# A fused mLSTM and FP4 feed-forward kernel: input rows of two batches in one transfer each, without copies of the inputs in DRAM

## The reference

```
q = layernorm(x); k = v = ctx
ig, fg = gates: [q, k, v] @ igate_w.T + igate_b, [q, k, v] @ fgate_w.T + fgate_b
log_f_cum = cumsum(log_sigmoid(fg)); log_D[s,t] = log_f_cum[s] - log_f_cum[t] + ig[t]  (t <= s)
D = exp(log_D - max_t log_D); C = (q k^T / 8) * D
h = C / (max(|sum C|, exp(-max)) + 1e-6) @ v; h = layernorm over each head * norm_w
x = x + h
z = layernorm(x); gate = fp4(z) @ fp4(w_gate).T; y = fp4(z) @ fp4(w_up).T      (512 -> 1408)
x = x + fp4(silu(gate) * y) @ fp4(w_down).T                                   (1408 -> 512)
```

## Time and profile before

| | |
|---|---|
| three runs | 2225.77, 2227.67, 2230.52 us (median 2227.67) |
| profiled execution | 2230.32 us, span in the trace 2228.6 us |
| mean granted TensorE clock | 0.902 of full speed |
| busy share of the span | PE 79%, DVE 81%, ACT 52%, POOL 55% |
| DMA | 647726 packets, 259.86 MB, mean 117 GB/s |

### The profile page before, as it was taken

One profiled execution on the slowest core, in us unless ns is written; L12 is line 12 of the kernel. 1 busy time (PEld: TensorE's weight loads), 2 busy tenths in 40 slices (PEclk: granted clock), 3 DMA queues, 4 the chain that ended last, 5 costly groups with the idle time before them and its releaser, 6 DMA issues. The chain is left out here.

```text
span 2228.6 us, 46871 instructions
## 1 busy us (share of the span) xinstructions
PE 1752.1 (79%) x16113; PEld 912.3 (41%) x16113; DVE 1811.8 (81%) x3327; ACT 1154.4 (52%) x2602; POOL 1220.3 (55%) x1260
## 2 busy tenths in 40 slices
PE   4444887869879696887869878686987869989998
PEld 3322443434434343443434444343443434444443
DVE  7953986959789695986969689595987959999996
ACT  7643553545555363563645456363554645655542
POOL 7843654636456463654546465463654646666663
PEclk8566988989989898998989989898999989999999
DMA  6395545546455564646545465554645545554333
GB/s 185 90 116 78 127 105 132 122 112 122 120 124 119 128 123 110 136 113 131 120 117 124 112 132 117 126 126 115 132 109 125 122 123 121 117 119 86 88 77 63
DMA packets 647726, 259.86 MB, mean 117 GB/s; under 512 B 581248, under 2 KB 603264, under 8 KB 646944
## 3 DMA queue, kind: packets, MB, share of 16 engines
q1 hardware_dynamic: 646672, 221.21, 48.6%
q10 hardware_dynamic: 816, 35.65, 3.8%
HBM read 159.22 MB, written 67.37 MB: 102 GB/s over the span
## 5 line engine op out<-in xcount | busy, mean ns | idle before, releaser
L592 PE MATMUL bank<-wgTh,xqT 128*128 128x512 f16 (+1 forms) x1536 | 579.7, 377 | 165.0 <-DMA xqT<-xqs 107.0
L592 PE MATMUL bank<-wuTh,xqT 128*128 128x512 f16 (+1 forms) x1536 | 578.0, 376 | 0.0
L1224 POOL TENSOR_TENSOR stage<-stage,hs 128x512 f32<-128x512 f32 (+1 forms) x192 | 213.4, 1111 | 304.4 <-DVE stage L1443 303.1
L592 PEld LDWEIGHTS bank<-wgTh,xqT 128*128 128x128 f16 x1536 | 155.0, 101 | 351.3 <-DMA xqT<-xqs 97.4
L592 PE MATMUL bank<-wgTl,xqT 128*128 128x512 f16 (+1 forms) x768 | 288.9, 376 | 0.0
L592 PE MATMUL bank<-wuTl,xqT 128*128 128x512 f16 (+1 forms) x768 | 288.2, 375 | 0.0
L748 PE MATMUL bank<-wdTh,work 128*128 128x512 f16 x704 | 269.8, 383 | 23.1 <-DMA work<-stage 22.6
L749 PE MATMUL bank<-wdTl,work 128*128 128x512 f16 x704 | 268.6, 382 | 0.0
L750 PE MATMUL bank<-wdTh,work 128*128 128x512 f16 x704 | 268.4, 381 | 0.0
L1279 POOL TENSOR_TENSOR stage<-stage,hinv 128x512 f32<-128x512 f32 (+1 forms) x192 | 210.5, 1109 | 30.7 <-DVE hinv L1542 24.1
L592 PEld LDWEIGHTS bank<-wuTh,xqT 128*128 128x128 f16 x1536 | 155.5, 101 | 154.4 <-issue 19.0
(11 more groups left out here) (215 smaller groups left out, 3978.2 us busy)
## 6 DMA issues: line engine op xcount, KB each, us to landing
wb<-warp_dram SPq DMA_DIRECT2D x256, 64.0 KB, 2.9
mb_D<-max_dram SPq DMA_DIRECT2D x128, 128.0 KB, 3.2
out_dram<-ob SPq DMA_DIRECT2D x128, 128.0 KB, 2.4
cn<-c_tiles SPq DMA_DIRECT2D x112, 128.0 KB, 2.9
xh_dram<-xb SPq DMA_DIRECT2D x55, 256.0 KB, 2.4
xzb<-xh_dram SPq DMA_DIRECT2D x220, 64.0 KB, 2.5
cf<-c_tiles SPq DMA_DIRECT2D x220, 64.0 KB, 2.5
xb<-x_tiles SPq DMA_DIRECT2D x52, 256.0 KB, 2.7
```

Of the source, the lines that this page charges most:

```text
L592: i = e.matmul(o[:, 0:width], x, w[:, c, n0:n0 + width], start=first and k < 2, stop=last and k >= 4)
L1224: e.tensor_tensor(blocks(hx[:, n0:n0 + w]), blocks(hx[:, n0:n0 + w]), per_block(hs2[:, n0 // BLOCK:(n0 + w) // BLOCK]), ALU.mult).then_inc ...
```

## The change

The DRAM copies `x_tiles` and `c_tiles`, the functions that make them and their counters go. `tokens(dram, t)` now gives both batches of a pair, [2, 64, 512], and each of `x_in`, `x1_in`, `stored` and the early `c_in` is a single transfer with it. The permuted `c_in` reads `ctx` itself, split by batch and by half of 32 rows instead of by the 32-column group: four transfers still, now each to all 128 partitions. `cn_in` is three transfers: parity 0 of both batches in one, parity 1 one for each batch. `mb_in` is one transfer of [2, 64, 512] with the row repeated over the 64 partitions, where it was two. For `wb`, the decay row in `warp_dram` is written one and a half times (its first half is repeated behind it), so that the two batches of a parity are consecutive for both parities, and two transfers read what four did.

```diff
@@ -94,13 +94,10 @@
 
     max_dram = nc.dram_tensor("max_dram", [NT // 4, GR * S2], F32, kind="Internal").ap()
     xh_dram = nc.dram_tensor("xh_dram", [2, P, E], F32, kind="Internal").ap()
-    warp_dram = nc.dram_tensor("warp_dram", [NT // 4, GR * S2], F32, kind="Internal").ap()
-
-    x_tiles = nc.dram_tensor("x_tiles", [NT, P, E], F32, kind="Internal").ap()
-    c_tiles = nc.dram_tensor("c_tiles", [NT, 3 * S2, E], F32, kind="Internal").ap()
-
-    def tokens(dram, t, b):
-        return dram[2 * t.p + b, t.chunk * S2:(t.chunk + 1) * S2, :]
+    warp_dram = nc.dram_tensor("warp_dram", [NT // 4, 3 * QR * S2], F32, kind="Internal").ap()
+
+    def tokens(dram, t):
+        return dram[2 * t.p:2 * t.p + 2, t.chunk * S2:(t.chunk + 1) * S2, :]
 
     with ExitStack() as stack:
         def sb(name, shape, dt=F32):
@@ -337,8 +319,7 @@
 
         def sp_stored(e, t):
             e.wait_ge(S_["out"], t.done())
-            for b in range(2):
-                e.dma_start(tokens(out, t, b), ob[t.parity][b * S2:(b + 1) * S2, :]).then_inc(s_stored[t.parity], 16)
+            e.dma_start(tokens(out, t), ob[t.parity][:, :]).then_inc(s_stored[t.parity], 16)
 
         def sp_x1_in(e, t):
             if t.at_start(2):
@@ -347,12 +328,7 @@
                 e.wait_ge(S_["w_xn"], 3 * NG)
             if t.has(4):
                 e.wait_ge(S_["out"], t.done(4))
-            if x_staged(t):
-                e.wait_ge(S_["x_tiles"], 32 * (t.chunk - 2))
-                e.dma_start(x1[t.slot % 4][:, :], x_tiles[t.first]).then_inc(s_x1_in[t.slot % 4], 16)
-                return
-            for b in range(2):
-                e.dma_start(x1[t.slot % 4][b * S2:(b + 1) * S2, :], tokens(x, t, b)).then_inc(s_x1_in[t.slot % 4], 16)
+            e.dma_start(x1[t.slot % 4][:, :], tokens(x, t)).then_inc(s_x1_in[t.slot % 4], 16)
 
         def sp_hqT(e, t, n):
             if t.at_start(0):
@@ -366,19 +342,13 @@
         def sp_x_in(e, t):
 
             if t.first < 4:
-                for b in range(2):
-                    e.dma_start(xin(t)[b * S2:(b + 1) * S2, :], tokens(x, t, b)).then_inc(S_["x_in"], 16)
+                e.dma_start(xin(t), tokens(x, t)).then_inc(S_["x_in"], 16)
                 return
             if not blocked(t.back(1)):
                 e.wait_ge(S_["x_T"], t.done(1))
             else:
                 e.wait_ge(S_["xh_out"], 16 * (t.first - 9))
-            if x_staged(t):
-                e.wait_ge(S_["x_tiles"], 32 * (t.chunk - 2))
-                e.dma_start(xb[:, :], x_tiles[t.first]).then_inc(S_["x_in"], 16)
-                return
-            for b in range(2):
-                e.dma_start(xb[b * S2:(b + 1) * S2, :], tokens(x, t, b)).then_inc(S_["x_in"], 16)
+            e.dma_start(xb[:, :], tokens(x, t)).then_inc(S_["x_in"], 16)
 
         def sp_xh_out(e, t):
             e.wait_ge(S_["xh"], t.done())
@@ -398,14 +368,13 @@
             if not blocked(t):
                 if t.has(1):
                     e.wait_ge(S_["c_T"], t.done(1))
-                for b in range(2):
-                    e.dma_start(cf[b * S2:(b + 1) * S2, :], tokens(ctx_in, t, b)).then_inc(S_["c_in"], 16)
+                e.dma_start(cf[:, :], tokens(ctx_in, t)).then_inc(S_["c_in"], 16)
                 return
             e.wait_ge(S_["cT"], t.done(1))
-            e.wait_ge(S_["c_tiles"], 48 * (t.chunk - 1))
-            rows = c_tiles[t.first][0:P, :].rearrange("(q s) (k g f) -> g s k q f", s=SQ, g=P // SQ, f=SQ)
-            for g in range(P // SQ):
-                e.dma_start(cf[g * SQ:(g + 1) * SQ, :].rearrange("s (k q f) -> s k q f", k=EC, f=SQ), rows[g]).then_inc(S_["cz_in"], 16)
+            rows = tokens(ctx_in, t).rearrange("b (q s) (k g f) -> b q g s k f", s=SQ, g=P // SQ, f=SQ)
+            for b in range(2):
+                for q in range(2):
+                    e.dma_start(cf[:, :].rearrange("p (k b q f) -> p b q k f", k=EC, b=2, f=SQ)[:, b, q], rows[b, q]).then_inc(S_["cz_in"], 16)
 
         def sp_mb_in(e, t):
             if t.at_start(0):
@@ -413,10 +382,8 @@
             if t.has(1):
                 e.wait_ge(S_["D"], t.done(1))
             e.wait_ge(S_["max_out"], t.dma(4))
-            for k in range(2):
-                at = (4 * k + t.p) * NH * S2
-                e.dma_start(mb[k * S2:(k + 1) * S2, :, :].rearrange("p h s -> p (h s)"),
-                            max_dram[t.chunk:t.chunk + 1, at:at + NH * S2].broadcast_to([S2, NH * S2])).then_inc(S_["mb_in"], 16)
+            row = max_dram[t.chunk, :].rearrange("(k n r) -> k n r", k=2, n=4)[:, t.p, :]
+            e.dma_start(mb[:, :, :].rearrange("p h s -> p (h s)"), row.unsqueeze(1).broadcast_to([2, S2, NH * S2])).then_inc(S_["mb_in"], 16)
 
         def sp_xqT(e, t):
             if t.at_start(0):
@@ -434,7 +401,9 @@
                 e.wait_ge(S_["gate"], t.quads_of(3, 2))
                 e.dma_start(max_dram[t.chunk, :].rearrange("(r s) -> r s", s=S2), mw[:, 0, :]).then_inc(S_["max_out"], 16)
                 e.wait_ge(S_["warp"], t.quads())
-                e.dma_start(warp_dram[t.chunk, :].rearrange("(r s) -> r s", s=S2), mw[:, 1, :]).then_inc(S_["warp_out"], 16)
+                again = warp_dram[t.chunk, :].rearrange("(r s) -> r s", s=S2)
+                e.dma_start(again[0:GR, :], mw[:, 1, :]).then_inc(S_["warp_out"], 16)
+                e.dma_start(again[GR:GR + QR, :], mw[0:QR, 1, :]).then_inc(S_["warp_out"], 16)
 
         def sp_wb_in(e, t):
             if t.at_start(0):
@@ -442,28 +411,21 @@
             if t.has(1):
                 e.wait_ge(S_["St_old"], t.done(1))
                 e.wait_ge(S_["xw"], t.done(1))
-            e.wait_ge(S_["warp_out"], t.dma(4))
+            e.wait_ge(S_["warp_out"], 2 * t.dma(4))
             for par in range(2):
-                for b in range(2):
-                    at = (((par ^ b) * 4 + t.p) * 2 + par) * HC * S2
-                    e.dma_start(wb[par * DH:(par + 1) * DH, b, :, :].rearrange("p c s -> p (c s)"),
-                                warp_dram[t.chunk:t.chunk + 1, at:at + HC * S2].broadcast_to([DH, HC * S2])).then_inc(S_["wb_in"], 16)
+                row = warp_dram[t.chunk, :].rearrange("(k n r i) -> k n r i", k=3, n=4, r=2)[par:par + 2, t.p, par, :]
+                e.dma_start(wb[par * DH:(par + 1) * DH, :, :, :].rearrange("p b c s -> p (b c s)"),
+                            row.unsqueeze(0).broadcast_to([DH, 2, HC * S2])).then_inc(S_["wb_in"], 16)
 
         def sp_cn_in(e, t):
             if t.has(1):
                 e.wait_ge(S_["vc"], t.done(1))
                 e.wait_ge(S_["st_mm"], t.done(1))
-            if c_staged(t):
-                e.wait_ge(S_["c_tiles"], 48 * (t.chunk - 1))
-                for par in range(2):
-                    e.dma_start(cn[:, :].rearrange("s (c r d) -> s r c d", r=2, d=DH)[:, par],
-                                c_tiles[t.first][par * S2:par * S2 + P, :].rearrange("s (c r d) -> s r c d", r=2, d=DH)[:, par]).then_inc(S_["cn_in"], 16)
-                return
-            for par in range(2):
-                for b in range(2):
-                    k = par ^ b
-                    e.dma_start(cn[k * S2:(k + 1) * S2, :].rearrange("s (c r d) -> s r c d", r=2, d=DH)[:, par],
-                                tokens(ctx_in, t, b).rearrange("s (c r d) -> s r c d", r=2, d=DH)[:, par]).then_inc(S_["cn_in"], 16)
+            to = cn[:, :].rearrange("p (c r d) -> p r c d", r=2, d=DH)
+            rows = tokens(ctx_in, t).rearrange("b s (c r d) -> r b s c d", r=2, d=DH)
+            e.dma_start(to[:, 0], rows[0]).then_inc(S_["cn_in"], 16)
+            for b in range(2):
+                e.dma_start(to[HALF[1 - b], 1], rows[1, b]).then_inc(S_["cn_in"], 16)
 
 
         def sp_w_in(e, m, b):
@@ -1065,27 +1027,8 @@
                     e.wait_ge(s_wtr[b % 4], 32 * (b // 4))
                 e.copy(wsp[b % 4][:, 0, :], group(m, b)).then_inc(S_["w_hi"], 1)
 
-        def act_stage_c(e, g):
-            if g > 2:
-                e.wait_ge(S_["c_tiles"], 48 * (g - 2))
-            at = slice(g * S2, (g + 1) * S2)
-            src = ctx_in[:, at, :].rearrange("(p b) s e -> b p s e", b=2)
-            for k in range(3):
-                e.dma_start(c_tiles[4 * g:4 * g + 4, k * S2:(k + 1) * S2, :], src[k % 2]).then_inc(S_["c_tiles"], 16)
-
-        def act_stage_x(e, g):
-            if g > 3:
-                e.wait_ge(S_["x_tiles"], 32 * (g - 3))
-            src = x[:, g * S2:(g + 1) * S2, :].rearrange("(p b) s e -> b p s e", b=2)
-            for k in range(2):
-                e.dma_start(x_tiles[4 * g:4 * g + 4, k * S2:(k + 1) * S2, :], src[k]).then_inc(S_["x_tiles"], 16)
-
         def act_turn(e, u):
             tn = Tile(u + 1)
-            g = (u + 3) // 4
-            if u % 4 == 1 and 4 * g < NT:
-                act_stage_x(e, g)
-                act_stage_c(e, g)
             t0 = Tile(u)
             t1 = Tile(u - 1)
             t2 = Tile(u - 2)
...
```

(34 more changed lines are left out.)

2 lines of the change are left out of this document (1 added, 1 removed).

## The result

The changed kernel takes 2839.75 us (median of 4 runs, 2835.43 to 2843.6); the kernel before took 2226.72 on the same chip. The ratio is 1.2752, 95% interval 1.2723 to 1.278: 613 us slower, where 863 were forecast. The direction, the range and the likeliest case were right; the size was too large.

What follows compares the result with a forecast made beforehand. Staging copies on 4 of 16 DMA engines stalled turns; new transfers on 2 or 4 engines would make engine 0 the bound. Sum: 2230.3 + 854 (turns) + 17 (tail) - 8 (start) = 3093, taken as 3090 us; range 2550 to 3620, likeliest 2750 to 3400 (0.62).

Steps and rivals of the forecast that it cites:

- The bound of before: Old kernel's turns: staging copies on 4 of 16 engines stall them, 230 us, plus 25 us at the start.
- Two and four engines: New transfers: DRAM outermost counts of 2 or 4 confine each to that many engines, always the same ones.
- Rival B: Row and context loads: only 2 KB rows confined, `cf` and `cn` spread; 40 us a turn, 2616 us, chance 0.13.
- Rival C: Confined transfers dearer and serialized: packets 108 and 22 ns, 60 us a turn, 3670 us, chance 0.09.
- The packets: Time per packet on one DMA engine: 92 ns for 2 KB, 12 ns for 128 B, 18 ns for 256 B.
- engine 0's sum: DMA engine 0 in a full turn: 23.6 rows, 4.6 `cn`, 6.1 `cf`, 10.7 spread transfers, 45.0 us together.
- In these 4 us engine 0 is empty: Each turn, from `xh_out` landing until `x_in` moves data: 2.4 plus 1.6 us idle, making 49 us a turn.
- Rival A: All transfers spread over 16 engines after all, so only staging's cost goes: 1975 us, chance 0.15.
- The start: Before the turns: -25 us from staging gone, +17 from first loads on 2 engines, -8 together.
- The tail: Last six turns, without input loads: engine 0 about 30 us a turn where 26.4 to 27.5 pass, +17 us.
- The marks: Expected in the new profile: q10 gone, period 45 to 52 us, DMA share about 0.3, GB/s near 70, PE 57%, DVE 59%.
- The small edits: SP's issue list: fewer issues, 2 us less a turn, and second warp row, all hidden; 0, ends -2 and 0 us a turn.

Runs made afterwards that it cites:

- swap_order: The changed kernel with x loads, output, decay rows and first ten context loads naming 64 tokens ahead of the two batches: 2098.59 us, ratio 0.9427 to the kernel before.
- micro: Computation left out, SP alone issues transfers in stages: eight 256 KB transfers took 43.8 us at outermost count 2, 9.0 with the order swapped.
- start_split: The changed kernel with only the first tiles' loads (x, residual's x, context) split per batch: 2781.6 us, ratio 1.2476 to the kernel before.
- mb_split: The changed kernel with the decay rows alone split into two transfers of 64 rows: 2639.29 us, ratio 1.1868 to the kernel before.
- rows_cn_split: The changed kernel with all rows and the first key/value load split per batch, context pieces left on 4 engines: 2019.27 us, ratio 0.9064 to the kernel before.
- spread_wb: The kernel before with both stagings spread, plus decay rows written one and a half times and read in two transfers: 2016.91 us against 2010.77.

## Why the prediction was right, and where its size was off

**The bound of before** was right. "Staging costs 230 us in the turns and 25 at the start": spreading it gave 197 and 28. Most of the difference is that the turn after a round of staging falls to 30.8 us on average and not to 27.5.

**Two and four engines** were right, the step on which everything stood (swap_order, micro). Rival B, with keys and context pieces spread, is out although the period of 43.0 us is near its 40: in micro the keys ran at 0.14 and the pieces at 0.29 of the engines, and splitting the keys gave 1.9 us a turn. Spreading the context pieces was not tried in the kernel. Rival C's 108 and 22 ns a packet are out by micro's prices (the 12900 engine-us in C's working of the 22 ns are what the small packets took; the larger ones took 4430).

**The packets** were somewhat too dear: 92, 12 and 18 ns forecast, 80, 11.4 and 16.5 measured alone. With the measured ones, in the old shares too (15.7 - 4.5 = 11.2), engine 0's sum is 20.5 + 4.2 + 5.8 + 11.2 = 41.7 us a turn in place of 45.0. This is the larger part of the excess: the turn is 43.0, not 49.

**"In these 4 us engine 0 is empty"** was too long as a term: 43.0 - 41.7 leaves 1.3. SP does wait for `xh_out` (1446.67 to 1449.89 in the turn above), but until it has landed the engines still move data. Behind it the trace shows all 16 idle (the window of 1449.70), in every one of the 53 turns, for 1.6 us on average by stretches of 0.25 us. Together: 53 x (43.0 - 32.9) = +536 where +854 was forecast.

**"Rival A holds while engine 0's work stays under 27 us"** failed. It made the cost a threshold; the steps of 3.1, 3.0, 5.5 and 1.9 us, and the 64 us of a single store in a kernel with room, show a price from the first confined transfer on, and 3 us rather than 4.5 even where engine 0 has most to do. Take the same prices off engine 0's sum step by step and it goes 41.7, 37.2, 32.7, 23.8, 20.1, while the turn goes 43.0, 39.9, 36.9, 31.4, 29.5: the gap grows from 1.3 to 9.4 us. So the sum comes near the turn only in the changed kernel. That engine 0 is the bound even there is not shown, since no row shows one engine by itself; what is shown is that the transposes behind confined transfers land late and are waited for.

**The start** had the wrong sign: -8 forecast, +42.3 measured, of which start_split gives back 59.6 by the mark. I priced the landings of loads that someone waits for (5.9 us each, three of them). What I left out is that SP is held in its next issue, whatever that carries. The front of the program is one list on that queue. The decay rows, which start_split leaves whole, have a part too: mb_split moves the mark by 18.9.

**The tail** was +17 forecast and +33.3 measured; all of it goes in rows_cn_split (253.1 against 255.0), so it is of the same cause. By the table the decay rows give 20.0 of it, the output 3.5, the residual's `x` rows 7.4 and the keys 4.2: the term fell short mostly at the decay rows.

**The marks.** q10 gone: yes. A period of 45 to 52: it was 41.3 to 45.5 (the first 36.4), alike in all four turns of a group. GB/s near 70: 79. DMA share about 0.3: it was 0.62 a turn. Around transposes that wait, the share goes above 1 while little moves (1.83 at 81 GB/s in the 4 us before the window of 0.13; in micro 1.67 at 53 GB/s behind the confined loads, 0.26 at 52 around the transpose alone), so I read their waiting on idle engines as counted busy; the share that shows confinement is that of a stretch with no transpose. PE 67% and DVE 65%, above the 57 and 59% of a longer span.

**The small edits** at nothing: spread_wb agrees for the decay rows of `wb`. **Rival A's 1975 us**, for a version without staging and with all transfers spread, was not run; with only the context pieces left on 4 engines it was 2019.
